# Sorting the last batch inside the attention programs of a two-layer kernel, as two units of four tiles

## What is computed

```python
def attn_a(x):                       # one head of 128, sigmoid instead of softmax
    q, k, v = x @ Wq.T + bq, x @ Wk.T + bk, x @ Wv.T + bv
    attn = sigmoid(layer_norm(q) @ layer_norm(k).T / sqrt(D) - log(S))
    return ((attn @ v) @ Wo.T + bo) * layerscale

def ffn(x):                          # 8 experts, the best 2 of each token
    xf = layernorm(x, ln_g, ln_b)
    scores, idx = top_k(xf @ router_w, 2)
    gate = softmax(scores)
    return sum over e of gate_e * expert_e(xf)
    # expert: z = layernorm(xf, eg, eb); clip(x1 * silu(clip(z @ W2 + b2))) @ Wo + bo,  x1 = z @ W1 + b1

x = x + attn_a(layernorm(x))
x = x + ffn(layernorm(x))
x = x + attn_b(layernorm(x))         # 16 heads of 64, running maximum over blocks of 64 keys
return x + ffn(layernorm(x))
```

## Time and profile before

| | us |
|---|---|
| median of 3 runs (lowest, highest) | 2641.01 (2637.9, 2643.7) |
| the profiled execution | 2635.07 |
| its span in the profile | 2633.3 |
| TensorE busy in the span | 2351.4 (89%) |
| VectorE busy | 2222.2 (84%) |
| ScalarE busy | 1647.1 (63%) |
| GpSimd busy | 1496.7 (57%) |

### The profile page before, as it was taken

How to read it: one execution, slowest core, us unless ns; L and a number is a source line. 1 busy time by engine, 2 the same in 40 slices (tenths; PEclk the granted TensorE clock), 3 DMA queues, 4 the chain that set the end, 5 groups by cost and what they waited for, 6 DMA issues and landing times. The chain is left out here.

```text
span 2633.3 us, 44081 instructions
## 1 busy us (share of the span) xinstructions
PE 2351.4 (89%) x15040; PEld 1791.6 (68%) x15040; DVE 2222.2 (84%) x4622; ACT 1647.1 (63%) x2850; POOL 1496.7 (57%) x1079
## 2 busy tenths in 40 slices
PE   5897499937999999999999999999999999929994
PEld 2454388824777777777777777777777777618883
DVE  6565477768999999999999999999999999647775
ACT  2355133335777777788878778787778877613333
POOL 0044444424666666667667766666866766723442
PEclk9897699968999999999999999999999999959997
DMA  8711366645345344434422333233323332015665
GB/s 199 205 65 40 112 190 189 187 116 134 87 100 131 89 97 106 120 81 100 92 71 68 84 84 79 60 76 80 97 62 76 84 79 49 16 61 174 187 192 158
DMA packets 171855, 281.36 MB, mean 107 GB/s; under 512 B 33356, under 2 KB 125394, under 8 KB 171632
## 3 DMA queue, kind: packets, MB, share of 16 engines
q1 hardware_dynamic: 161968, 259.58, 38.5%
q0 software_dynamic: 9664, 18.97, 2.1%
HBM read 118.41 MB, written 63.31 MB: 69 GB/s over the span
## 5 line engine op out<-in xcount | busy, mean ns | idle before, releaser
L2178 POOL TENSOR_TENSOR b_prob<-b_prob,b_weight 128x1024 f32<-128x1024 f32 x512 | 958.3, 1903 | 506.2 <-DVE b_weight L2138 506.0
L2108 DVE TENSOR_REDUCE b_bmax<-b_score 128x16 f32<-128x1024 f32 x512 | 620.8, 1213 | 44.0 <-PE b_score L1963 27.5
L2061 ACT ACTIVATE b_prob<-b_score,b_neg_m 128x1024 f32<-128x1024 f32 x512 | 581.1, 1135 | 77.2 <-DVE b_neg_m L2116 76.8
L2095 DVE TENSOR_REDUCE b_bsum<-b_prob 128x16 f32<-128x1024 f32 x512 | 605.6, 1202 | 0.0
L2047 ACT ACTIVATE b_pT<-b_turn 128x512 f32<-128x512 f32 x1024 | 560.1, 609 | 62.7 <-PE b_turn L1976 57.2
L1976 PE MATMUL b_turn<-ident,b_prob 128*128 128x128 f32 x4096 | 531.2, 273 | 3.2 <-ACT b_pT L2047 3.2
L1976 PEld LDWEIGHTS b_turn<-ident,b_prob 128*128 128x128 f32 x4096 | 477.1, 140 | 74.9 <-ACT b_pT L2047 3.3
L1963 PE MATMUL b_score<-b_KH,b_QS 128*128 128x512 f32 x1024 | 479.1, 468 | 16.4 <-ACT b_prob L2061 14.5
L1943 PE MATMUL b_acc<-b_pT,b_V 128*64 128x256 f32 x4096 | 470.3, 382 | 0.0
L1963 PE MATMUL b_score<-b_KL,b_QS 128*128 128x512 f32 x1024 | 405.8, 396 | 0.0
L1943 PEld LDWEIGHTS b_acc<-b_pT,b_V 128*64 128x64 f32 x4096 | 282.7, 137 | 151.0 <-issue 21.6
(11 more groups left out here) (313 smaller groups left out, 2956.8 us busy)
## 6 DMA issues: line engine op xcount, KB each, us to landing
f_e_w<-f_weights SPq DMA_DIRECT2D x78, 776.0 KB, 4.6
f_sorted<-zeros SPq DMA_DIRECT2D x172, 193.5 KB, 5.2
b_KH<-b_k_high SPq DMA_DIRECT2D x128, 256.0 KB
b_KL<-b_k_low SPq DMA_DIRECT2D x128, 256.0 KB
b_QS<-b_q_high SPq DMA_DIRECT2D x64, 256.0 KB, 3.7
b_QS<-b_q_low SPq DMA_DIRECT2D x64, 256.0 KB, 4.9
b_hb<-b_hT SPq DMA_DIRECT2D x31, 512.0 KB
f_e_z<-f_sorted SPq DMA_DIRECT2D x78, 129.0 KB, 2.2
```

The costliest lines, as they stand in the source:

```text
L2061: act.activation(prob[r % 4][k][:], score[k % 2][:], ACT.Exp, bias=neg_m[r % 2][:, k:k + 1]).then_inc(prob_ready, 1)
L2095: dve.tensor_reduce(bsum[r % 2][:, k, :], prob[r % 4][k][:].rearrange("p (n c) -> p n c", c=KV_BLOCK), AX, ALU.add).then_inc(sum_ready, 1)
L2108: maxima = chain.mark(dve.tensor_reduce(bmax[r % 2][:, k, :], score[k % 2][:].rearrange("p (n c) -> p n c", c=KV_BLOCK), AX, ALU.max))
L2178: pool.tensor_tensor(tile, tile, weight[r % 2][:, k, :].unsqueeze(2).to_broadcast([P, NB, KV_BLOCK]), ALU.mult).then_inc(scaled, 1)
```

## The change

The last batch is no longer sorted after the attention. `Sorter` now knows five units: three of eight tiles (batches 0 to 2) and two of four tiles (rows 0 to 3 and 4 to 7 of batch 3; units 3 and 4). `sort_tokens` and `gated_experts` are gone; the block table and the gates are made by a class `BlockTable` at the end of the attention programs, with the same instructions as before.

In layer 0:
- In batch 3 all eight steps of query half 0 come first, then those of half 1 (`place_of`). Half 0 is copied out at u = 8 and projected back at u = 9, half 1 at the end, so four tiles of `X` are final half a batch before the others. The fold's products in batch 3 stand at u = 2 instead of 6 (`FOLD_IN`).
- Unit 2 is turned, routed and copied at u = 7 to 10, its two roots stand at u = 3 and u = 13 (the second together with unit 3's first), its first four z rows at u = 15 and the other four behind the last product.
- The z rows of units 0 and 1 are made at the end of the batch in which they are routed, instead of at u = 1 and 2 of the next one.
- For units 3 and 4 VectorE makes the normalised rows, the gain and the shift (`vector_rows`, `vector_gain`) in place of ScalarE and GpSimd; ScalarE makes z and copies it into a second buffer (`scalar_second_z`), which gets the numbers of choice 1, so no scatter waits for another to land.
- GpSimd's gain and shift of unit 2 come between the two choices of unit 1's scatters. All scatters are inside this program.
- SyncE issues the second 43 clears behind the load of expert 3.

In layer 1: unit 3 is measured, turned, chosen and routed in the last slots (END = 128; `tensor_end`, `scalar_end`, `vector_end`), in PSUM banks and SBUF arrays that the softmax no longer uses; unit 4 and the table follow behind the last slot (the `_rest` functions). ScalarE loads the Sqrt table at slot 128. The two columns of gain and shift are loaded in this layer too.

```diff
+        def place_of(b, u):
+            return (u // 2, u % 2) if b + 1 < BATCH else (u % TPB, u // TPB)
...
-                for k in range(2):
-                    sorter.pool_number(pool, 1, k)
-                    sorter.pool_scatter(pool, 1, k, 0, TPB)
+                sorter.pool_number(pool, 1, 0)
+                sorter.pool_scatter(pool, 1, 0, 0, TPB)
                 sorter.pool_gain(pool, 2)
                 sorter.pool_shift(pool, 2)
+                sorter.pool_number(pool, 1, 1)
+                sorter.pool_scatter(pool, 1, 1, 0, TPB)
+                for k in range(2):
+                    sorter.pool_number(pool, 2, k)
+                    sorter.pool_scatter(pool, 2, k, 0, TPB)
+                for n in (3, 4):
+                    sorter.pool_number_both(pool, n)
+                for n in (3, 4):
+                    sorter.pool_scatter_both(pool, n)
+                sorter.pool_end(pool)
```

```diff
+                def sort_in_last(u):
...
+                    if u == 7:
+                        sorter.turn(pe, 2, 0, ring[0])
+                    if u == 8:
+                        sorter.route(pe, 2, 0, ring[0])
+                        sorter.turn(pe, 2, 1, ring[1])
+                    if u == 9:
+                        project_back(BATCH - 1, 0)
+                    if u == 10:
+                        sorter.route(pe, 2, 1, ring[1])
+                    if u == 15:
+                        pe.wait_ge(sorter.logits_taken, sorter.halves(3))
+                        sorter.count(pe, 2, ring[0])
```

```diff
+                def sort_in_last(u):
+                    if u == 3:
+                        sorter.root(act, 2, 0)
+                    if u in (4, 5):
+                        sorter.scalar_rows(act, 2, u - 4)
+                    if u == 7:
+                        sorter.copy_turned(act, 2, 0, ring[0][:])
+                    if u == 8:
+                        copy_out(BATCH - 1, 0)
+                        sorter.copy_turned(act, 2, 1, ring[1][:])
+                    if u == 13:
+                        sorter.root(act, 2, 1)
+                        sorter.root(act, 3, 0)
+                    if u == 15:
+                        sorter.scalar_z(act, 2, 0)
...
+                sorter.scalar_z(act, 2, 1)
+                sorter.copy_turned(act, 3, 0, ring[1][:])
+                sorter.root(act, 3, 1)
+                sorter.root(act, 4, 0)
+                sorter.scalar_z(act, 3, 0)
+                sorter.scalar_second_z(act, 3)
```

```diff
+                def last_batch():
+                    update(BATCH - 2)
+                    tokens_to_sort(2)
+                    fold_biases(BATCH - 1)
+                    invert(2, 0)
+                    sorted_rows(2)
+                    update_half(BATCH - 1, 0)
+                    tokens_to_sort(3)
+                    for half in range(2):
+                        sorter.take_logits(dve, 2, half, ring[half])
+                    sorter.pick(dve, chain, 2)
+                    invert(2, 1)
+                    invert(3, 0)
+                    sorter.vector_rows(dve, 3)
+                    sorter.find_slots(dve, chain, 2, ring[0])
+                    sorter.vector_gain(dve, chain, 3)
+                    sorted_rows(3)
+                    update_half(BATCH - 1, 1)
+                    tokens_to_sort(4)
+                    sorter.take_logits(dve, 3, 0, ring[1])
+                    sorter.pick(dve, chain, 3)
+                    invert(3, 1)
+                    invert(4, 0)
+                    sorter.vector_rows(dve, 4)
+                    sorter.find_slots(dve, chain, 3, ring[1])
+                    sorter.vector_gain(dve, chain, 4)
+                    sorted_rows(4)
+                    sorter.take_logits(dve, 4, 0, ring[0])
+                    sorter.pick(dve, chain, 4)
+                    invert(4, 1)
+                    sorter.find_slots(dve, chain, 4, ring[0])
+                    table.vector(dve, chain)
```

```diff
-            if e < 2:
-                clear.sync(sp, e, 2)
+            if e == 0:
+                clear.sync(sp, 0, 2)
...
             if e + 2 < EXPERTS:
                 load(e + 2)
+            if e == 1:
+                clear.sync(sp, 1, 2)
```

```diff
+UNITS = ((0, TPB), (TPB, TPB), (2 * TPB, TPB), (3 * TPB, TPB // 2), (3 * TPB + TPB // 2, TPB // 2))
+WHOLE = 3
+BUFFERS = ((0, 1, 2, 0, 1), (0, 0, 0, 1, 0))
+HATS = ((0, 0, 0, 1, 0), (None, None, None, 0, 1))
...
+    def vector_gain(self, dve, chain, n):
+        self.loads(dve)
+        dve.wait_ge(self.normal, self.number(n) + 1)
+        self.buffer_free(dve, n)
+        spread = lambda v: v[:].unsqueeze(1).to_broadcast([P, self.tiles(n), D])
+        chain.link(dve.tensor_tensor(self.data(n), self.hats[n], spread(self.gain), ALU.mult))
+        self.xf_made = chain.mark(dve.tensor_tensor(self.data(n), self.data(n), spread(self.shift), ALU.add))
...
+    def pool_scatter_both(self, pool, n):
+        m = self.number(n)
+        pool.wait_ge(self.z_ready, m + 1)
+        pool.wait_ge(self.slots_ready, m + 1)
+        self.pool_scatter(pool, n, 0, 0, self.tiles(n))
+        pool.wait_ge(self.z_copied, (len(UNITS) - WHOLE) * self.layer + n - WHOLE + 1)
+        self.pool_scatter(pool, n, 1, 0, self.tiles(n))
```

```diff
+    def pool_rest(self, pool, turned):
+        s = self.sorter
+        pool.wait_ge(turned, 8 * (self.END - 2))
+        self.table.pool_consts(pool)
+        for n in (3, 4):
+            s.pool_number_both(pool, n)
+        for n in (3, 4):
+            s.pool_scatter_both(pool, n)
+        s.pool_end(pool)
...
+    def tensor_end(self, pe, sl, k, prob_ready):
+        s, bank = self.sorter, self.banks[0]
+        if sl == self.END + 2 and k == 1:
+            pe.wait_ge(prob_ready, 4 * self.END)
+            s.turn(pe, 3, 0, bank[0])
+        if sl == self.END + 2 and k == 3:
+            s.route(pe, 3, 0, bank[0])
...
+    def scalar_end(self, act, sl, k):
+        s = self.sorter
+        if sl == self.END and k == 3:
+            s.load_root_table(act, 2)
+        if sl == self.END + 1 and k == 2:
+            s.root(act, 3, 0)
+        if sl == self.END + 2 and k == 2:
+            s.copy_turned(act, 3, 0, self.banks[0][0])
+        if sl == self.END + 2 and k == 3:
+            s.root(act, 3, 1)
...
+    def vector_end(self, dve, chain, sl, k, wo_taken):
+        if sl == self.END + 1 and k == 3:
+            self.measure_tokens(dve, chain, 3, wo_taken, self.END - 2)
+        if sl == self.END + 2 and k == 0:
+            self.normal_tokens(dve, chain, 3)
+        if sl == self.END + 3 and k == 0:
+            self.choose(dve, chain, 3, self.banks[0][0])
+    def vector_rest(self, dve, chain, wo_taken):
+        s = self.sorter
+        self.measure_tokens(dve, chain, 4, wo_taken, self.END)
+        s.find_slots(dve, chain, 3, self.banks[0][1])
+        self.normal_tokens(dve, chain, 4)
+        self.choose(dve, chain, 4, self.banks[1][0])
+        s.find_slots(dve, chain, 4, self.banks[1][1])
+        self.table.vector(dve, chain)
```

935 lines of the change are left out of this document (461 added, 474 removed).

## The result

The changed kernel takes 2611.41 us (median of 4 runs, 2610.9 to 2612.07), the kernel before beside it 2642.36 (4 runs, 2637.9 to 2644.89): a ratio of 0.9891, interval 0.9878 to 0.9904. Forecast were 2599 and a range of 2591 to 2611. The direction was right, the size was not: 31 us gained in place of 42. The profiled execution took 2612.07 us, span 2610.4. Against the profiled execution of before (span 2633.3) that is only 22.9; where the other 8 went is the subject of the second experiment.

What follows compares the result with a forecast made beforehand. Two sort programs of about 50 us each, nearly idle on TensorE, plus a 10.54 us load wait, were taken as the bound. Layer 0 -25.7 and layer 1 -16.0 sum to -41.7: 2593.4, plus 5.9 to the median, 2599; range 2591 to 2611.

Steps and rivals of the forecast that it cites:

- Part 1: Layer 0, batches 1 and 2: clears moved behind expert 3's load, so batch 3 starts 16.5 us earlier (bounds 12 and 17.5).
- The slow stretch with it: Batch 1 of layer 0: TensorE's half-clock stretch goes together with its 10.54 us wait, saving 1.74 and 2.55 us.
- what is late next?: Batch 1, once the load wait goes: ScalarE's table and VectorE's q and k rows are early enough; no wait from VectorE.
- the 137 that the prediction named as a sign of being wrong: Layer 0: the forecast would be wrong if batch 2 starts later than 137 us.
- Part 2: Layer 0's last batch sorted inside the attention: unit 2's numbering 10.0 us earlier from batch 3's start; two more numberings add 0.8.
- S + 36.6: Layer 0: TensorE's last attention product starts near 36.6 us after the start of batch 3, where it was 39.8 before.
- The slower rival: Tails of both layers: VectorE holds up 48 scatters; at twice their spacing, 61 us more, ending at 2660; chance 0.04.
- I keep each: Gaps from last scatter to experts' first load stay as before: 6.6 us in layer 0, 5.1 in layer 1.
- Part 3: Layer 1's tail: last X 1.7 us later, last slots 5.9 earlier, eight scatters (10.1) saved; -16.0 us, bounds -12 and -18.
- The offset: Whole kernel: the profiled execution lay 5.9 us below the runs' median, so 5.9 was added to 2593.4, giving 2599.3.
- the fold loads gain nothing: Layer 0, batch 1 or 2: something else holds it, only the other two parts' gains stay, 2616; chance 0.10.
- small units starve GpSimd: Four-tile units' hand-overs run late: 0.7 us at each of six in layer 1, 3 in layer 0; 2606 to 2608; chance 0.17.

Runs made afterwards that it cites:

- the second run: The changed kernel with GpSimd's folds of experts 4 and 5 moved behind the scatters of unit 0: 2615.74 us, ratio 0.9889.
- Clears only: The kernel before with only the second 43 clears moved behind the loads of expert 3: 2630.89 us against 2643.59, ratio 0.9955.

## Second question: the last slots, and the execution that the prediction was made from

**Unit 3 behind the slots.** The changed kernel, with what was put inside slots 129 to 131 of layer 1 (statistics, root, turning, routing, choice of unit 3) taken out and done behind them:

```diff
-                        late.tensor_end(pe, sl, k, prob_ready)
-                        late.scalar_end(act, sl, k)
-                        late.vector_end(dve, chain, sl, k, wo_taken)
...
+                late.measure_tokens(dve, chain, 3, wo_taken, late.END - 2)
+                late.normal_tokens(dve, chain, 3)
+                late.choose(dve, chain, 3, late.banks[0][0])
                 late.vector_rest(dve, chain, wo_taken)
```

> The changed kernel with layer 1's work for unit 3 taken out of the last slots and put behind them, in front of unit 4's. Theory A (the in-slot instructions themselves hold up TensorE and ScalarE): slots 128 to 131 take 24.6 us again from X update to X update, as before the change, instead of 30.9; the slots of unit 4 come 27 us behind the last X update, the end 3 to 5 us later than in the changed kernel: about 2615. Theory B (the 4.6 us lost in slot 130 is something of the program's layout or of that one execution): they still take about 29, and the time is about 2619.

Measured: 2623.2 (4 runs), ratio 0.992 (0.9904 to 0.9937). The last four updates of X lie at 2266.85, 2275.69, 2289.17 and 2298.11: 31.3 us with no work of the sort in them, as long as with it (30.9). That is theory B, so nearly all of the table's +6.3 doesn't come from the change. The work inside the slots is worth 11 us, more than either theory gave: the slots of unit 4 come at 2325.89 in place of 2314.79.

**Before again.** The kernel before, unchanged, profiled once more.

> The kernel before, unchanged, profiled a second time. Question: is the profiled execution that the prediction was made from (2635.07 us, X updates of the last slots at 2283.97, 2292.66, 2301.38 and 2308.54, 24.6 us, granted clock 1.00 to the end) like the other executions, whose median is 2641 to 2644? Theory: it was not. In all five other profiles so far the third of the last slots takes 13.0 to 13.7 us in place of 8.7, with TensorE's product of 32 matmuls lasting some 6.5 us, and the granted clock falls behind it. So a second profile shows these three intervals with one of 12.7 to 13.7 us, some 30.5 to 31.5 us from the first of the last four updates to the last, and a span near 2640. Rival (the change itself, or the moved clears, bring the long slot): 24.6 us again, and a time near 2635.

Measured: 2640.5 us, and these updates of X:

```profile
2284.78 0.43 DVE L2131 TENSOR_TENSOR X<-b_misc,X 128x256 f32<-128x256 f32 x1 [0.31 <-PE b_misc L1988]
2293.56 0.42 DVE L2131 TENSOR_TENSOR X<-b_misc,X 128x256 f32<-128x256 f32 x1 [8.15 <-PE b_misc L1988]
...
2306.95 0.42 DVE L2131 TENSOR_TENSOR X<-b_misc,X 128x256 f32<-128x256 f32 x1 [12.97 <-remote]
2314.90 0.42 DVE L2131 TENSOR_TENSOR X<-b_misc,X 128x256 f32<-128x256 f32 x1 [7.53 <-PE b_misc L1988]
```

The intervals are 8.8, 13.4 and 8.0 us. In the profile that the prediction rests on they were 8.7, 8.7 and 7.2, while of the 125 intervals ahead of the last two all but the first agree within 0.1 us in the two profiles. So the execution that the prediction rests on was 5.5 us faster than this one, and the long slot alone is 5.6. Batch 3 of layer 0 also started 2.9 us later here, at 201.1, because in batch 2 the clock was at half behind the bias products, but by the experts' first load only 1.4 of that was left, and smaller differences cancel it. The size fits the 5.9 us between that execution's time and the median, which the prediction carried over as an unexplained offset. That its other runs had the long slot is not shown, since they have no profile. Against this second profile the change of the spans is 2638.8 - 2610.4 = 28.4, near the 31 of the medians, and the last slots are only 0.75 us longer (30.12 against 30.87). The start of batch 3 moved by 201.1 - 184.5 = 16.6. That this is the forecast 16.5 is luck: batch 2 was 3.4 us longer here than in the rows that the forecast was made from.

**The clock held.** Is the long slot a matter of TensorE having too little to do? The changed kernel, with one more matmul in each quarter of the last slots:

```diff
+                        if sl >= late.END:
+                            if sl == late.END and k == 0:
+                                pe.wait_ge(prob_ready, 4 * late.END)
+                            pe.matmul(late.banks[1][1], QS[1][0][:, 0:P], KH[1][0][:, 0:HALF], start=True, stop=True)
```

> The changed kernel with one more matmul of 512 columns (attention weights' type, into a free part of PSUM) in every quarter of the last slots, 16 or so in all, behind the transposes, where TensorE waits 0.2 to 0.6 us for ScalarE. The scores, which every slot before has, have ended there. Theory C (the clock falls in the last slots because TensorE has less work in them than in the slots before): with more work the clock stays, the third of the last slots takes about 9 us in place of 13.5, the last X update comes 3 to 5 us earlier, counted from the expert load, and the median is 2607 to 2609. Rival D (TensorE is held in another way, or the clock falls whatever it does there): the long slot stays, and each matmul adds up to 0.21 us: 2611 to 2615.

Measured: 2613.17 (4 runs), ratio 0.9909 (0.9888 to 0.993), and intervals of 10.5, 13.6 and 11.1 us. The theory falls: the long slot stays, and the others grow by what was added. What the profiles show of it: TensorE issues the 32 matmuls of slot 130 at the usual pace, but ScalarE, which waits for the last of them, goes on 3 us late. In the changed kernel:

```profile
2279.91 3.67 PE L2093 MATMUL b_acc<-b_pT,b_V 128*64 128x256 f32 x32
...
2286.63 0.38 ACT L2193 ACTIVATE b_oT<-b_acc 128x256 f32<-128x256 f32 x1 [5.97 <-remote]
```

Half speed would give such a delay, but that is not shown: the granted clock reads 1.00 during these matmuls, and falls to 0.50, if at all, only some us later (with the added matmuls from about 2285.8, in the profile just shown not before 2295). Why it happens stays open.

**Changed kernel again**, unedited, on one chip with two others that are told of below (**The same again**, **And the fold later**).

> The changed kernel, unchanged, beside the two that follow. In the three profiles of the call before this one the third of layer 1's last slots took 9.0 us, not 13.0 to 13.7 as in the eight profiles ahead of it. Theory K (the long slot goes with the chip, or its condition at the time): all three profiles of this call show it, or none does; with it the changed kernel takes about 2611, without it about 2604. Rival L (it comes and goes between executions): the three differ among themselves.

Measured: 2609.82 (4 runs) against 2642.9, ratio 0.9881 (0.9858 to 0.9904). All three profiles taken on this chip have the long slot (13.5, 13.1 and 13.6 us), and none of the three on the chip of **Order and wait** had (9.0 each). On four chips with three or four profiles each, all of a chip agreed: the slot goes with the chip or its condition at the time (theory K), not with the single execution. The time of a chip doesn't go with it as closely. The kernel before took 2632.65 on the chip without the slot and 2642.9 here, but 2635.98 on the chip of **Before again**, all of whose profiles have it; the slot itself is worth 4.5 us.

## Third question: the gap behind the last scatter

In the kernel before 6.57 and 5.16 us passed from the end of the last scatter to the experts' first load. In the changed kernel it is 9.26 and 9.22.

**SyncE waits.** The wait for the landing of the last rows is taken from GpSimd and given to SyncE:

```diff
-                sorter.pool_end(pool)
...
                 fold.sync(sp, clear)
+                sorter.pool_end(sp)
```

> The changed kernel with one edit: the wait for the last scatters to land, at the end of both attention programs, is made by SyncE instead of GpSimd. Theory A (part of the 9.3 us from the last scatter's end to the first load of the experts is GpSimd leaving its long program after that wait): the gap falls by about 2 us in each layer, to some 7.3, and the time to about 2607. Theory B (the gap is landing plus what SyncE does itself behind the barrier): both gaps stay at 9.2 to 9.3 us, and the time at 2611.

Measured: gaps of 7.70 and 7.73; 2611.67 (4 runs), ratio 0.9872 (0.9854 to 0.989). So 1.5 us of each gap are that wait in front of GpSimd's leaving, less than the 2 of theory A. The rest is something else. What the edit does to the time these runs don't show: the changed kernel wasn't run on this chip, its ratio elsewhere (0.9891, 0.9878 to 0.9904) overlaps, and in this profile the last slots took 34.3 us in place of 30.9, which is as much as both gaps gave.

**Tail in its own program.** The last unit's scatters, the wait and the block table in a short program behind each attention program:

```diff
-                for n in (3, 4):
-                    sorter.pool_scatter_both(pool, n)
-                sorter.pool_end(pool)
+                sorter.pool_scatter_both(pool, 3)
...
+        with nc.Block() as block:
...
+            def _(pool):
+                sorter.pool_scatter_both(pool, 4)
+                sorter.pool_end(pool)
```

> The changed kernel, with the last unit's 16 or 8 scatters per copy, the wait for their landing and the block table taken out of both attention programs into a short program of their own behind each. Question: why are there 9.2 us between the last scatter and the experts' first load, where the short sort programs of before showed 6.6 and 5.2? Theory E (leaving a long program costs more than leaving a short one): the two gaps fall to 5.0 to 6.6 us, and the border that is new costs 2 to 5 us between two scatters. The sum is nothing to 2 us either way: 2609 to 2614. Rival F (the gap comes from what stands between last scatter and end, such as the wait on three semaphores by GpSimd or the landing of the rows): both gaps stay at 8.5 to 9.5 us, and the border adds its cost: 2615 to 2622.

Measured: 2611.48 (4 runs), ratio 0.9903 (0.9881 to 0.9926). The gaps fall to 4.81 and 4.49, a little below the 5.0 to 6.6 of theory E, and the new border costs 5.6 us between two scatters, a little above its 2 to 5:

```profile
260.95 0.96 POOL L946 DMA_INDIRECT f_sorted<-l_again,l_slots  x1 [0.30 <-issue]
267.55 0.96 POOL L946 DMA_INDIRECT f_sorted<-l_rows,l_slots  x1 [5.63 <-PEq L566]
...
276.39 0.96 POOL L946 DMA_INDIRECT f_sorted<-l_again,l_slots  x1 [0.30 <-issue]
...
282.16 0.42 SPq L1535 DMA_DIRECT2D f_e_z<-f_sorted  x1
```

Theory E (the long program) holds, but "long" could be its code or its transfers. Put in a row by what GpSimd had issued in the program that ends, the gaps suggest the second.

**More transfers, more code.** The changed kernel with 32 transfers more, or with 160 memsets more, of GpSimd in layer 0, ahead of unit 2's numbering; layer 1 is left as it is.

```diff
+                for i in range(32):
+                    pool.dma_start(spare_dram[i * P:(i + 1) * P, :], zeros.tile[:, 0:WITH_ID]).then_inc(spare_moved, 16)
+                pool.wait_ge(spare_moved, 32 * 16)
```

```diff
+                for i in range(160):
+                    last = pool.memset(spare[:, i:i + 1], 0.0)
+                last.then_inc(spare_moved, 16)
+                pool.wait_ge(spare_moved, 16)
```

> The changed kernel with 32 more transfers issued by GpSimd in layer 0's attention program, ahead of the numbering of unit 2, from zeros to spare memory. The whole is slower by some 25 to 35 us, which is not what is looked at; the gap from layer 0's last scatter to the experts' load is. Gaps so far against transfers that GpSimd had issued in the program that ends: 8: 4.8 and 4.5; 16: 5.1; 32: 6.6; 80: 9.3 and 9.2. Theory G (leaving a program costs GpSimd more, the more transfers it issued there): 10.5 to 11.5 us in layer 0 with 112, and 9.2 in layer 1, where nothing is changed. Rival H (it is another trait of a long program, such as the length of its code or its other engines): 9.0 to 9.6 in layer 0.

> The changed kernel with 160 more small memsets of GpSimd in layer 0's attention program, at the same place as the 32 transfers of the run before. Theory G (number of transfers): the gap behind layer 0's last scatter stays at 9.2 us. Rival H (length of GpSimd's code): it grows beyond 9.6. The whole is slower by 5 to 15 us, which is not what is looked at.

(The counts in the first text were mine and wrong: each layer scatters 64 times, not 80, so it is 64 in the changed kernel, with 4 stores more in layer 1, and 96 here.) With more transfers:

```profile
277.24 0.96 POOL L939 DMA_INDIRECT f_sorted<-l_again,l_slots  x1 [0.30 <-issue]
...
290.07 0.42 SPq L1532 DMA_DIRECT2D f_e_z<-f_sorted  x1
```

With more code:

```profile
269.70 0.96 POOL L940 DMA_INDIRECT f_sorted<-l_again,l_slots  x1 [0.30 <-issue]
...
279.91 0.42 SPq L1533 DMA_DIRECT2D f_e_z<-f_sorted  x1
```

11.87 and 9.25 us; in layer 1 both show 9.2. So theory G: what counts is how many transfers GpSimd has issued in the program that it leaves. All gaps, where GpSimd both scatters last and waits: 8 transfers 4.81 and 4.49; 16 transfers 5.16, 4.94 and 4.96; 32 transfers 6.57, 6.59 and 6.57; 64 transfers 9.25 to 9.44 (68: 9.22 to 9.25); 96 transfers 11.87. That is 3.9 + 0.083 for each: 4.6, 5.2, 6.6, 9.2, 11.9. The formula is a line through these points and no more; the four stores of layer 1 don't lengthen its gap. The points with 8 to 32 transfers come from short programs and those with 64 and 96 from long ones, but the step from 64 to 96 is within one program, and it gives the same price (2.6 us for 32). What GpSimd does in this time the traces do not show. (The whole took 2613.19 and 2603.43 us, one run each, beside a before of 2632.65 on that chip.)

## Fourth question: the way to unit 2's numbering, and a better version

**Order and wait.** The changed kernel with SyncE's wait, and in layer 0 ScalarE's pair of roots one unit earlier, both halves of unit 2's z rows in the last two units, the count one unit earlier, and unit 2's slots ahead of unit 3's first steps on VectorE:

```diff
-                    if u == 13:
+                    if u == 12:
                         sorter.root(act, 2, 1)
                         sorter.root(act, 3, 0)
-                    if u == 15:
-                        sorter.scalar_z(act, 2, 0)
+                    if u in (14, 15):
+                        sorter.scalar_z(act, 2, u - 14)
...
                     invert(2, 1)
+                    sorter.find_slots(dve, chain, 2, ring[0])
                     invert(3, 0)
                     sorter.vector_rows(dve, 3)
-                    sorter.find_slots(dve, chain, 2, ring[0])
```

> The changed kernel with the numbering of unit 2 prepared earlier in layer 0 (the pair of square roots one unit earlier, z rows in the last two units ahead of the copy of the attention product, the count one unit earlier, VectorE's slots of unit 2 ahead of the first steps of unit 3), and with SyncE in place of GpSimd waiting for the last rows to land in both layers. Theory: the 4.5 us that the prediction lost between the start of batch 3 and unit 2's numbering lie in what ScalarE does there, and about 1.7 of them are to be had this way: numbering 40.9 us behind the start of batch 3 in place of 42.56; the two gaps from the last scatter to the experts' load are 7.7 us in place of 9.2, as they were when SyncE alone was changed. Sum 1.7 + 2 x 1.5 = 4.7: 2606.7. Rival: numbering waits for the slots or TensorE instead and stays at 42 or more, and the median is 2608.5 to 2611.

Measured: 2597.02 (4 runs) against 2632.65 on that chip, ratio 0.9862 (0.9838 to 0.9887). Batch 3 starts at 183.70, and:

```profile
214.53 1.28 ACT L998 ACT_TABLE_LOAD   x1
...
218.60 1.64 ACT L1047 ACTIVATE l_rows<-l_rows,l_bias,l_rstd 128x128 f32<-128x128 f32 x4
...
220.79 1.64 ACT L1047 ACTIVATE l_rows<-l_rows,l_bias,l_rstd 128x128 f32<-128x128 f32 x4
...
223.18 0.14 POOL L905 IOTA l_rows<- 128x8 f32 x1 [7.64 <-DVE l_slots L1184]
```

Numbering 39.5 us behind the start of batch 3 in place of 42.56, so 3.1 and not 1.7 us, and both gaps are 7.7. z was ready at 222.4; now the slots come last, at 223.0. The 2597.02 can't be laid beside the 2606.7 of the theory, since this chip is also faster for the kernel before and has no long slot; the next run settles the gain.

**The same again**, beside the changed kernel on one chip.

> The version with the earlier numbering of unit 2 and SyncE's wait a second time, now beside the changed kernel itself. From the profiles its scatters start 3.1 us earlier, counted from the start of batch 3, and each gap is 1.5 us shorter: 6.1 us below the changed kernel of this call, if nothing in layer 1 eats it up; if layer 1 does, 3 us or less.

Measured: 2605.3 (4 runs), ratio 0.9863 (0.984 to 0.9885), against 2609.82 of the changed kernel: 4.5 us less, where 6.1 or at most 3 were expected (the four runs are 2604.6 to 2609.2 against 2608.7 to 2613.9). Numbering came 41.2 us behind the start of batch 3 in this profile, against 42.6 in the changed kernel's on this chip; the gaps are 7.70 and 7.73. In layer 0 only 1.2 us are left at the experts' first load, because batch 3 started 1.6 us later than in the changed kernel's profile, the one without the 3 us wait.

**And the fold later.** The same version, with the edit of the second run on top.

> The same version with GpSimd's folding of experts 4 and 5 behind the scatters of unit 0. Alone, that brought batch 3 of layer 0 forward by 3.7 us, and the gain was gone before unit 2's numbering. Theory M (it was gone because TensorE's products came late and its clock fell in that one profile): numbering now comes 39.5 us behind the start of batch 3, at some 219.5, and the median is 3 to 4 us below the version without it. Rival N (something that is always there, such as GpSimd's folding now standing beside another part of VectorE's work, eats it): numbering at 222 to 224 and no difference over 1.5 us.

Measured: 2604.34 (4 runs), ratio 0.9852 (0.983 to 0.9874). Batch 2 starts at 133.22 and batch 3 at 181.41, 2.9 us earlier than without it (and 1.3 earlier than in the changed kernel's profile on this chip), and numbering is at 223.51 against 225.49: 2 us of it arrive. In the median 1 us is left, which the runs (2602 to 2606.7 against 2604.6 to 2609.2) can't tell from nothing. So the numbering lies between theory M and rival N, and for the time N has it: the earlier start of batch 2 is real, but the folding now stands beside VectorE's work of batch 2 and holds that up. Sixteen steps that take 4.19 us in the earlier trace rows take twice as long:

```profile
161.65 8.39 DVE L455 TENSOR_SCALAR a_qkv<-a_qkv,a_qk_norm_both,a_qk_norm_rstd 128x128 f32<-128x128 f32 x16
```

TensorE then waits 1.89 us at 178.18 for VectorE's choice, and 1.42 at 218.51 for ScalarE. By its ratio this is the fastest version, though it can't be told from the one without the later fold. That one is 4.5 us ahead of the changed kernel on the one chip where both ran.

## Why the forecast was 12 us too low

The spans miss by 41.7 - 22.9 = 18.8 us. Of these, 6.6 are in how far the two profiled executions lie from their medians (5.9 below, 0.7 above); the other 12 are the miss of the median. By the steps of the prediction:

- **Part 1**, start of batch 3: -13.7 in place of -16.5. That the load lands in time and that the 10.54 us go was right. Two steps failed. "The slow stretch with it": 1.9 us of half clock stay in batch 1, behind the bias products, and another 1.8 come in batch 2, where the profile of before had none (others of the changed kernel have it there or not). And "what is late next?" was answered by when VectorE's instructions had ended before, as if they took as long beside GpSimd's gain, shift and fold: 3.02 us of wait and 1.7 of half clock behind it came in. A 2.13 us wait for ScalarE at the end of batch 1, which the prediction didn't count, went. Together batch 1 is 11.9 us shorter in place of 14.8 and batch 2 0.5 in place of 1.7; the wait for the choice at its end did go. Batch 1 also started 1.25 us earlier (86.17 in place of 87.42), which is chance: over all profiles that start lies between 85.5 and 87.5. Batch 2 began at 137.07, past the 137 that the prediction named as a sign of being wrong.
- **Part 2**, the way to numbering: -7.3 in place of -10.0. All of the miss lies ahead of the last attention product, which starts 39.2 us behind the start of batch 3 in place of 36.6; what follows it takes the forecast 3.3. About 1 us is arithmetic: the prediction names some 1 us of wait for the two roots at unit 13 (0.96 measured) and leaves it out of S + 36.6. Another 1.3 are two waits for ScalarE's sigmoid that were put at nothing, 0.27 and 1.03 us, the second behind normalised rows for which ScalarE had waited 0.89 us for VectorE. The remaining 0.4 is in small pieces. The 4.12 us for the choice went, half the back projection cost 1.05 (0.9). Moving ScalarE's and VectorE's steps got 3.1 us back in one profile and 1.4 in another.
- **The scatters**: 43.76 us, predicted 43.5. Neither slots nor VectorE held one up. The slower rival is refuted.
- **The gaps**, "I keep each": +2.7 and +4.1. This is the largest error of mechanism, 6.8 us. The prediction took the leaving of a program as a constant; it grows with the transfers that GpSimd has issued in it. The merged programs have 64 where the sort programs had 32 and 16: 32 x 0.083 = 2.7 and 48 x 0.083 = 4.0. That GpSimd's leaving of the long program was hidden behind the attention's end before is argued, not measured.
- **Part 3**, layer 1: the chain from the last X to the slots takes 16.4 us (to 2314.96), predicted 16.8, and 18.3 are saved behind the last X, predicted 17.7. From the update in slot 128 to the last one it takes 6.3 us more, predicted 1.7. In profiles without the long slot this stretch is 24.6 us before and 26.3 in the better version of this kernel, which is that 1.7; with it, it is 30.1 before and 30.9 after. The rest is the long slot, which the profiled execution of before didn't have.
- **The offset**: adding 5.9 came out about right in size, and the long slot would account for it. That was luck, since no cause was looked for. It hid that the rows came from an untypical execution, and without it the forecast would have been further off.
- Rivals: "the fold loads gain nothing" is out (12.7 us alone); of "small units starve GpSimd" layer 1 shows nothing; in layer 0 z of unit 2 is 2.7 us late, by the waits under part 2.
- Not explained: 0.5 us in the middle and 1.7 us in layer 1's experts. The same stretches of the other profiles spread wider than that (1982.8 to 1988.4, and 272.5 to 277.5).

## What to carry to other kernels

Merging two programs moves a border rather than removing it: ask which engine leaves last, what it must clear up, and whether that was hidden so far. When a wait goes, look at what the engine that is late next has beside it, not only at when it ended before; GpSimd's large element-wise steps stretch VectorE's small ones to their own length. A slow stretch that follows a wait need not go when the wait goes: price it by itself. And where the profiled execution lies outside the range of the other runs, as 2635.07 below 2637.9 did, find the place before building a sum on its rows, by a second profile if there is one.

## What the runs showed of the hardware

- From the end of GpSimd's last scatter to the next program's first load it takes about 3.9 us plus 0.083 for each transfer that GpSimd issued in the program that ends (8 to 96 transfers, 4.5 to 11.9 us), 1.5 of it the wait for the last rows; 160 more memsets change nothing (9.25).
- A VectorE step of 0.17 us took 2.28, 2.05 and 1.81 beside GpSimd's element-wise steps of 2.36, 2.17 and 1.90; statistics were not stretched (eight took 1.64 beside one of 1.89 in **Clears only**, at 124.92), nor was a reduction of 0.22. Scatters beside VectorE kept 1.265 us from start to start.
- Right behind 32 fp32 matmuls of one column each (3.63 us) TensorE's granted clock read 0.50 to 0.78 over the next 4.3 us (107.7 to 112.0) in all thirteen profiles in which TensorE went on without a wait there. In batch 2 it fell in some profiles (0.82 from 154 to 163 in the changed kernel) and not in others (1.00 in **Tail in its own program**).
- TensorE's 32 fp32 matmuls of 3.67 us end some 3 us late in one slot, at a granted clock that reads 1.00. Eleven profiles show it and four don't, and those of one chip agree. The interval between two updates of X is 13.0 to 13.9 us with it and 8.7 to 9.0 without.
